# A two-layer gated mixer on one core: the first network, its norms and the attention products moved into the scan of the next batch, and the next mixer's preparation placed between the gate and the second network's down products

## What is computed

```python
# layer 0, mixer: a selective scan over 512 positions, 512 channels, 16 states
x  = silu(conv4(in_proj(ctx)))              # 512 channels x 512 positions
dt = softplus(dt_proj(x_proj(x)[:16]) + b)
state = state * exp(dt * A) + (dt * x) * B  # one sequential scan per channel and state
y  = sum_over_states(state * C) + D * x
x1 = x_in + tanh(g_x[0]) * y * silu(z)      # z is the layer norm of x_in
# layer 0, first network: 512 -> 2048 -> 512, weights of -1, 0, 1, inputs rounded to 8 bits
x2 = x1 + tanh(g_f[0]) * w2(round8(gelu(w1(round8(layernorm(x1))))))
# layer 1, attention over channels, its weights are made from ctx
x3 = x2 + tanh(g_x[1]) * layernorm(x2) @ attention.T
# layer 1, second network in fp32: 512 -> 2048 -> 512
out = x3 + tanh(g_f[1]) * (proj2(gelu(proj1(layernorm(x3)) + b1)) + b2)
```

## Time and profile before

| what | value |
|---|---|
| median of 3 runs | 1172.61 us (1170.66 to 1172.63) |
| the profiled execution | 1169.88 us, its span 1168.1 us |
| PE busy | 828.8 us (71%) |
| DVE busy | 904.9 us (77%) |
| ACT busy | 639.3 us (55%) |
| POOL busy | 563.9 us (48%) |
| mean granted TensorE clock | 0.844 of full speed |
| DMA | 130.07 MB, mean 111 GB/s |

### The profile page before, as it was taken

How to read it: one execution, slowest core, us unless ns; L and a number is a source line. 1 busy time by engine, 2 the same in 40 slices (tenths; PEclk the granted TensorE clock), 3 DMA queues, 4 the chain that set the end, 5 groups by cost and what they waited for, 6 DMA issues and landing times.

```text
span 1168.1 us, 10659 instructions
## 1 busy us (share of the span) xinstructions
PE 828.8 (71%) x2665; PEld 405.5 (35%) x2704; DVE 904.9 (77%) x1151; ACT 639.3 (55%) x889; POOL 563.9 (48%) x462
## 2 busy tenths in 40 slices
PE   5342311298598875899599877889498868887998
PEld 2010100143243332444234333344233323344886
DVE  3889988977888899687888899688878898565333
ACT  5556856467368843275488642365388641432442
POOL 0487568122777665123786674023877673123000
PEclk8565555599789997998799988998699988998999
DMA  7055995000168696220188786300287775200222
GB/s 249 0 106 110 218 260 100 16 1 1 43 139 176 147 228 152 94 86 36 29 173 177 159 199 162 128 0 36 45 179 162 164 185 146 90 1 1 91 91 72
DMA packets 51439, 130.07 MB, mean 111 GB/s; under 512 B 6304, under 2 KB 7456, under 8 KB 50864
## 3 DMA queue, kind: packets, MB, share of 16 engines
q0 software_dynamic: 17280, 62.92, 29.1%
q1 hardware_dynamic: 34096, 66.53, 16.9%
HBM read 62.33 MB, written 4.19 MB: 57 GB/s over the span
## 4 chain that ended last, share of the span: by engine, by line
PE 43%; DVE 22%; issue 12%; POOL 9%; DMA 7%; ACT 6%; POOLq 0%; DVEq 0%; ACTq 0%; SPq 0%; another core or an unknown queue 0%
PE bank L582 12%; DVE pair L1124 7%; PE bank L595 7%; DMA u<-work 6%; POOL work L1508 5%; PE bank L610 4%; PE pair L610 4%; PE pair L526 3%; PE pair L513 2%; PE bank L444 2%; DVE work L1128 2%; PE pair L571 1%; PE bank L452 1%; PE bank L469 1%; DVE u L1135 1%
## 5 line engine op out<-in xcount | busy, mean ns | idle before, releaser
L1124 DVE TENSOR_TENSOR_SCAN pair<-pair,work 128x512 f32<-128x512 f32 x256 | 313.0, 1223 | 49.1 <-ACT pair L797 42.7
L1508 POOL TENSOR_TENSOR work<-du,bcast 128x1024 f32<-128x1024 f32 x128 | 318.3, 2489 | 67.4 <-DMA u<-work 61.8
L797 ACT ACTIVATE pair<-dt,a_neg 128x512 f32<-128x512 f32 x256 | 168.1, 685 | 65.8 <-DVE work L1128 48.4
L582 PE MATMUL bank<-stage,ring 128*128 128x512 f32 x384 | 180.9, 615 | 22.2 <-ACT hx L979 8.0
L1128 DVE TENSOR_TENSOR work<-pair,ccast 128x512 f32<-128x512 f32 x256 | 177.0, 691 | 14.6 <-ACT bcast L782 1.4
L1519 POOL DMA_DIRECT2D u<-work x120 | 113.8, 950 | 81.2 <-DVE work L1128 74.6
L595 PE MATMUL bank<-ring,stage 128*128 128x512 f32 x192 | 94.5, 644 | 41.3 <-DVE stage L1365 39.9
L418 PE MATMUL bank<-xd,pick 128*128 128x512 bf16 x108 | 49.5, 458 | 96.8 <-ACT bcast L782 67.7
L582 PEld LDWEIGHTS bank<-stage,ring 128*128 128x128 f32 x384 | 74.3, 197 | 116.4 <-issue 89.8
L1554 POOL TENSOR_SCALAR stage<-stage,fst 128x2048 f32<-128x2048 f32 x16 | 33.1, 2067 | 119.8 <-DVE fst L1333 119.8
L782 ACT ACTIVATE bcast<-bank 128x512 f32<-128x512 f32 x64 | 38.0, 594 | 76.0 <-POOL work L1508 51.9
(11 more groups left out here) (158 smaller groups left out, 1578.6 us busy)
## 6 DMA issues: line engine op xcount, KB each, us to landing
u<-work POOLq DMA_DIRECT2D x120, 512.0 KB, 5.2
ring<-ffn_dram SPq DMA_DIRECT2D x144, 256.0 KB, 3.6
ring<-ffn_dram SPq DMA_DIRECT2D x16, 512.0 KB, 3.3
xres<-x_dram SPq DMA_DIRECT2D x4, 1024.0 KB, 5.4
stage<-w_dram SPq DMA_DIRECT2D x1, 4096.0 KB, 17.1
stage<-w_dram SPq DMA_DIRECT2D x4, 1024.0 KB, 8.4
out_dram<-stage SPq DMA_DIRECT2D x16, 256.0 KB, 2.8
ctxT<-ctxT_dram SPq DMA_DIRECT2D x4, 512.0 KB, 7.4
```

The costliest lines, as they stand in the source:

```text
L582: last = pe.matmul(banks[2 + f % 2][:], up_slot(f)[:, k * P:(k + 1) * P], xnT[:, k, :], start=k == 0, stop=k == J - 1)
L797: act.activation(pairs[s % DECAYBUFS][:, q, :], dt[:, p * HALF + q, :], ACT.Exp, scale=a_neg[:, p * HALF + q, n:n + 1]).then_inc(s_decay, 1)
L1124: dve.tensor_tensor_scan(state, state, row, 0.0, ALU.mult, ALU.add).then_inc(s_scan, 1)
L1508: pool.tensor_tensor(work[:, s % SCANBUFS, :, :], du[:, p * HALF:(p + 1) * HALF, :], bcast[:, n % 2, :].unsqueeze(1).broadcast_to([P, HALF ...
```

## The change

The tiles and the arithmetic stay; the order on each engine, and which PSUM banks are used, change. A pass is now `pass_(b, m, nxt)`. The part called `chain` (first network, norms and attention products of batch b) stands at places (5, 0) to (8, 0), one or two steps behind each half step of the scan of batch m. The 16 `f_up` move to places (8, 2) to (12, 1), and the 16 `f_down` units to (12, 2), (12, 3) and 14 places of a new part, `end(b, m, nxt)`. `end` holds the gate of batch m, these units, and the preparation of batch nxt with both halves of its state 0, then `up1` and `gelu1` of block 0. `up1` has two banks in turn where it had three, and shares them with `transpose_h`, `norm_transpose` and `attend`. The passes are now: preparation of batch 0; scan of batch 0, whose `end` prepares batch 1; a loop of two passes; a pass with b = 2 and m = 3, whose `end` prepares nothing; and the last with batch 3 alone. `quantise` writes its normalised rows into `xn` and no longer into `ccast`.

```diff
-SCAN_SLOTS = {4: (0, None), 5: (1, 2), 6: (3, 4), 7: (5, 6), 8: (7, 8), 9: (9, 10), 10: (11, 12), 11: (13, 14), 12: (15, None)}
-QK_SLOT = 5
-ATT_SLOTS = {6: 0, 7: 1, 8: 2, 9: 3}
-ATT_LAST_SLOT = 10
+SCAN_SLOTS = {5: (1, 2), 6: (3, 4), 7: (5, 6), 8: (7, 8), 9: (9, 10), 10: (11, 12), 11: (13, 14), 12: (15, None)}
+QK_SLOT = 7
+ATT_SLOTS = {8: 0, 9: 1, 10: 2, 11: 3}
+ATT_LAST_SLOT = 12
 ZSTAT_SLOT = 10
 ZS_SLOT = 12
-GATE_SLOT = 13
-QUANT_SLOT = 14
+END_SLOT = 13
...
-ATT_BANKS = (4, 6, 7, 6)
-MEAN_BANK = 1
-DT_BANKS = (0, 1, 5, 6)
-
-FFN_UP = {(5 + f // 4, f % 4): f for f in range(FT)}
-FFN_DOWN = {(9, 0): (0, 0), (9, 1): (0, 2), (9, 3): (0, 4),
-            (10, 0): (0, 6), (10, 1): (0, 8), (10, 3): (0, 10),
-            (11, 0): (0, 12), (11, 1): (0, 14),
-            (12, 0): (1, 0), (12, 1): (1, 2), (12, 3): (1, 4),
-            (13, 0): (1, 6), (13, 2): (1, 8), (13, 3): (1, 10),
-            (14, 0): (1, 12), (14, 3): (1, 14)}
-FOURTH_SLOTS = {(11, 1): 0, (14, 1): 1}
+MEAN_BANK = 2
+DT_BANKS = (5, 6, 7, 4)
+PROJ_BANKS = (6, 7)
+GATE_BANKS = (1, 0, 4, 5)
+NORM_ORDER = (0, 1, 4, 2, 5, 3, 6, 7)
+
+FFN_UP = {at: f for f, at in enumerate([(8, 2), (8, 3)] + [(slot, place) for slot in (9, 10, 11) for place in range(4)]
+                                       + [(12, 0), (12, 1)])}
+FFN_DOWN = {at: (i // 8, i % 8 * 2) for i, at in enumerate([(12, 2), (12, 3)] + [(END_SLOT, i) for i in range(14)])}
...
                 if j == 0:
                     pe.wait_ge(s_ctx, b * 16 + 16)
                     if prev is not None:
-                        pe.wait_ge(s_x1, prev * T + T)
-                elif j == 1 and prev is not None:
-                    pe.wait_ge(s_qT, prev * T + T)
+                        pe.wait_ge(s_hc, (prev + 1) * HN * HALF)
                 elif j >= 2:
                     pe.wait_ge(s_inprojc, b * J + j - 1)
                 for k in range(KC):
-                    last = pe.matmul(banks[j % 2][:], ipw[:, k, j * P:(j + 1) * P], ctxT[:, k, :],
+                    last = pe.matmul(banks[PROJ_BANKS[j % 2]][:], ipw[:, k, j * P:(j + 1) * P], ctxT[:, k, :],
                                      start=k == 0, stop=k == KC - 1)
...
+                    if c >= 2 or t == 1:
+                        pe.wait_ge(s_gelu, b * T * FC + g - 1)
+                    elif t >= 2:
+                        pe.wait_ge((s_ev0, s_ev1)[c], b * T + t - 1)
+                    elif c == 0:
                         pe.wait_ge(s_x4, b * T + 1)
                     for k in range(J):
-                        last = pe.matmul(banks[4 + g % 3][:], qT[:, k, t * P:(t + 1) * P],
...
-                    pe.wait_ge(s_x2, b * T + T)
-                if t == T - 1:
-                    pe.wait_ge(s_x3, b * T + 2)
+                elif t < T - 1:
+                    pe.wait_ge(s_ev0, b * T + t + 2)
+                else:
+                    pe.wait_ge(s_x3, b * T + t)
                 for k in range(J):
-                    last = pe.matmul(banks[ATT_BANKS[t]][:], xnT[:, k, t * P:(t + 1) * P], attT[:, k, :],
+                    last = pe.matmul(banks[2][:], xnT[:, k, t * P:(t + 1) * P], attT[:, k, :],
                                      start=k == 0, stop=k == J - 1)
                 last.then_inc(s_xm, 1)
...
+            def chain(b, slot, place):
+
+                if (slot, place) == (5, 0):
+                    up1(b, 1)
+                if (slot, place) == (5, 1):
+                    transpose_h(b, 0)
+                    down1(b, 0)
+                if (slot, place) == (5, 2):
+                    up1(b, 2)
...
+                if (slot, place) == (6, 0):
+                    up1(b, 3)
                     norm_transpose(b, 0)
+                    attend(b, 0)
+                if (slot, place) == (6, 1):
...
+                units(0)
+                if m is not None:
+                    gate_transposes(m, (0, 1))
+                units(1)
+                if m is not None:
+                    gate_transposes(m, (2, 3))
+                if nxt is not None:
+                    project(nxt, m, 0)
+                    project(nxt, m, 1)
...
+                units(5)
+                if nxt is not None:
+                    if m is None:
+                        pe.wait_ge(s_const, const_wait)
+                        pe.wait_ge(s_ones, 2)
+                    low_rank(nxt, m)
...
+                units(7)
+                if nxt is not None:
+                    scan_bcast(nxt, 0, 0)
+                    scan_bcast(nxt, 1, 0)
+                units(8)
+                if nxt is not None:
+                    scan_bcast(nxt, 0, 1)
+                units(9)
+                if nxt is not None:
+                    scan_bcast(nxt, 2, 0)
+                    scan_bcast(nxt, 1, 1)
+                units(10, 11, 12, 13)
...
+            end(None, None, 0)
+            pass_(None, 0, 1)
+            with pe.Fori(0, B - 2) as i:
+                pass_(i, i + 1, i + 2)
+            pass_(B - 2, B - 1, None)
+            pass_(B - 1, None, None)
...
+                    softplus(nxt, m)
+                    first_copy(nxt, m, 0, 0)
+                    first_copy(nxt, m, 1, 0)
+                if m is not None:
+                    q_copy(m, 3)
+                if nxt is not None:
+                    first_copy(nxt, m, 0, 1)
+                    decays(nxt, 0, 0)
+                    copy_bc(nxt, 2, 0)
+                    copy_bc(nxt, 1, 1)
+                    decays(nxt, 0, 1)
+                if m is None:
+                    weights(4)
+                if m is not None:
...
+            def chain(b, slot, place, last):
+
+                if (slot, place) == (5, 0):
                     dve_f.start()
-                if scans:
+                    h_scale(b, 0)
+                if (slot, place) == (5, 1):
+                    h_quant(b, 0)
+                    h_scale(b, 1)
+                if (slot, place) == (5, 2):
+                    h_quant(b, 1)
+                if (slot, place) == (5, 3):
+                    second(b, 0)
+                    h_scale(b, 2)
...
+            def end(b, m, nxt):
+
+                if m is not None:
+                    gate(m, 0)
+                    if b is None:
+                        weights(END_SLOT)
+                    gate(m, 1)
+                    for t in range(T):
+                        first_sum(m, t)
+                if nxt is not None:
+                    convolve(nxt, 0)
+                if m is not None:
+                    quantise(m, 0)
...
+                if b is not None:
+                    fourth(b, 0)
...
+                    softplus_max(nxt)
+                    softplus_tmp(nxt)
+                    softplus_sum(nxt, 0)
+                    softplus_sum(nxt, 1)
+                    half_step(nxt, 0, 0)
+                    half_step(nxt, 0, 1)
+                if b is not None:
+                    fourth(b, 1)
```

More of the change, by code:

```diff
@@ new lines, in chain @@
+                if (slot, place) == (6, 2):
+                    h_quant(b, 3)
+                    norm_apply(b, 4)
+                    second(b, 2)
+                if (slot, place) == (6, 3):
+                    third(b, 1)
+                    norm_apply(b, 2)
+                if (slot, place) == (7, 0):
+                    norm_apply(b, 5)
+                    second(b, 3)
+                if (slot, place) == (7, 1):
+                    third(b, 2)
+                    norm_apply(b, 3)
```

797 lines of the change are left out of this document (355 added, 442 removed).

## The result

| | before | after |
|---|---|---|
| median | 1172.62 us | 1287.28 us (1286.81 to 1290.51) |
| ratio | | 1.0988, 95% interval 1.0967 to 1.1009 |
| span of the profiled execution | 1168.1 us | 1285.0 us |
| mean granted TensorE clock | 0.844 | 0.836 |

The account below looks back on a forecast made before the run. No engine is full; the limit changes by stage. Stretch changes of -45.0, +94 in scans, -74, +37.0 and +4.5 put +16.4 on 1168.0 us, a 1184.4 span; with time around it and the median offset, 1189 us, range 1160 to 1220.

Parts of the forecast that it names:

- What bounds the kernel, and the cuts: Whole span: no engine full, limit changes by stage; cut at each scan's end and first half step of state 1.
- First end, last end, start and tail: Batch 1's preparation after a scan 71.6 us; batch 3's gate with units 69.5; opening 208.4; closing second network 94.4.
- DVE floor of S, 155 us: State 1 to scan's end, three times: DVE's 120.1 us scan plus 34.9 network work; with waits 169, ends 161 to 180.
- New waits inside the network are small when I follow block by block: Network inside the scan: only two new waits found, 0.7 us at first h_scale and 0.8 at last second.
- ScalarE pays 7.7 us beside DVE work, and I cost it at nothing: Each scan: six gelu1-related table loads of 1.28 us, hidden beside DVE work; 7.7 us if that cover is gone.
- 6 us for GpSimd: Each scan: norm_apply and h_quant slowed when meeting GpSimd in memory, 6 us taken from a possible 0 to 22.8.
- ScalarE holds the decays: In scans, ScalarE waits for TensorE before decays; six of twelve places cost 2.1 us, time 1227; chance 0.13.
- the floor: Rival: DVE never waits in a scan except three table waits, scan stretch 161 us, total 1165; chance 0.22.
- the case of no net effect: Whole kernel: gains of 119 us and losses of 136 cancel if a tenth of losses fails, 1172; chance 0.07.
- The signs named beforehand: Forecast wrong if scans stay under 163 us, or scan's end to next state 1 is far over 87.
- C, 82 us: Scan's end to next state 1, twice: TensorE bound, 74.8 us work plus waits of 4, 2 and 1.5; ends 76 to 87.
- Network alone, 69.5: Batch 3's network by itself: shared banks 2 and 3 make it 69.5 us in place of 65.0, ends 65 to 73.

Follow-up runs that it names:

- a1: Changed kernel with each spread of the next place issued on TensorE ahead of the part that waits for ScalarE: 1261.2 us, ratio 1.0781.
- a2: Changed kernel with eight extra thrown-away products on TensorE between transpose_h and down1: 1266.7 us, ratio 1.0839.
- a3: Changed kernel with gelu1 as a scaling without Gelu, so no table load for it; computation left out: 1258.2 us, ratio 1.0735.
- c1: a1 with each down1 moved one place later, behind the h_copy of its block: 1247.4 us, ratio 1.0692.
- c2: c1 with units 10 and 11 issued ahead of two spreads in the stretch from scan's end to next state 1: 1234.6 us, ratio 1.0588.
- b1: Changed kernel with the first part of the change undone, all of chain running before slot 5 of the scan: 1319.1 us, ratio 1.1323.
- i2: c2 with norm_apply as two operations of two tensors, all operands in SBUF: 1251.9 us, ratio 1.0700.

## Why the prediction was wrong, point by point

- **What bounds the kernel, and the cuts:** right. First end, last end, start and tail came out within 4.2 us each. The two ends were sums over one engine with waits found by name; start and tail were carried over from the trace before.
- **DVE floor of S, 155 us:** right; DVE was busy 156.6 to 163.4.
- **"New waits inside the network are small when I follow block by block":** this is the step that failed. I followed `down1` to `second` and `gelu1` to `h_scale`, each block's own data. I did not follow the scan's data through the same queues: the spread behind `down1` on TensorE, its copy ahead of the decays on ScalarE, `h_copy` behind them. I had 0.7 and 0.8 us of new waits and 8.2 of idle time in all; the trace has 33 us idle in the network part. The edits that attack it, a1, a2, a3 and c1 (which contains a1), took 14, 7, 12 and 14 us off the second S. All in all c2 takes 43 of the 85.5 us off the three S, and leaving out the table loads 11 more; the last 31, some 10 per S, no run took away.
- **"ScalarE pays 7.7 us beside DVE work, and I cost it at nothing":** wrong twice; there are seven loads, 9.0 us, and S was 10.0 shorter without them (a3). The price had been named for the case that the cover is gone, and in the relay it was.
- **TensorE's clock in S:** no term for it. `down1` took 5.3 to 6.6 us in the second S in place of 3.6. The fillers brought 8 us per S back.
- **6 us for GpSimd:** near enough as work: VectorE's busy time is 2 to 8 us over the floor in after, and in c2 `norm_apply` takes 12.4 instead of 4.4 us. How much of it is on the path in after no run shows. As a rival for the whole gap it falls by that busy time, and by c2, whose S is 18 us shorter with longer hold-ups.
- **Rival "ScalarE holds the decays":** the nearest in kind, since it let ScalarE wait for TensorE before the decays; I had given it 0.13. It was priced at 2.1 us for six of twelve places, a row in which ScalarE only loads a table. The waits of ScalarE here are 5.5 to 7.0 us, because they hold a whole `down1` or `attend`.
- **The other rivals and the signs:** the floor and the case of no net effect needed shorter scans than the forecast and fall with S of 194 to 200. The signs named beforehand, S under 163 or C far over 87, did not include the way it came: S over its upper end of 180 three times.
- **C, 82 us:** the mechanism was right, the term mis-sized. TensorE in the first C, around the two spreads:

```profile
529.14 0.39 PE L416 MATMUL bank<-xd,pick 128*128 128x512 bf16 x1 [3.87 <-ACT bcast L792]
529.37 5.29 PE L589 MATMUL bank<-ring,stage 128*128 128x512 f32 x8
...
542.34 0.39 PE L416 MATMUL bank<-xd,pick 128*128 128x512 bf16 x1 [3.82 <-ACT bcast L792]
542.57 8.73 PE L589 MATMUL bank<-ring,hT 128*128 128x512 f32 x16
```

  The first wait is the 4 predicted. The second is 3.8, not 2, and behind each the next units run at the lower clock, 1.6 and 1.7 us longer than the 3.65 and 7.03 that as many products take elsewhere in this C.
- **Network alone, 69.5:** 74.9, and 75.4 in b1. With two banks, `transpose_h`, `h_copy` (2.0 us) and `down1` stand in line. VectorE is as busy there as before, 41.5 us; its waits before `third` for the attention product grew from 4.4 to 12.1 us, and those before `h_scale` for `gelu1` from 4.5 to 9.1. No run tests which of the shared banks makes them.
- **Open too:** how much of the last 14 us of S in c2 (183 on average against 169) is GpSimd's hold-up. No run took it away; i2 only shows that adding to it costs. And `up1` with two PSUM banks instead of three: in the part with the network TensorE stood 12.1 us for `gelu1` before a chunk of `up1` in the second S of after, and no run gave the third bank back.

## What to carry to other kernels

When work is moved beside other work, walk the orders of two engines that feed each other, not one block's data: for each wait of engine A on B, ask what stands ahead of the awaited instruction in B's order, and what that in turn waits for. If the answer comes back to A, the two take turns, and busy shares of all engines stay low while the time grows. What helps is to issue the small thing that the other engine needs first (here one spread of 0.4 us) ahead of the large one; the price of a term such as a table load can be nothing under cover (the first S of c2) and full in a relay (10.0 us for seven loads of 1.28).

## What the runs showed of the hardware

- Eight more products before each `down1`, thrown away, shortened the kernel by 1.4% (1.0988 to 1.0839); `down1` went from 6.15 to 3.61 us at the place shown, and the second S from a granted clock of 0.86 to 0.90.
- A product of two tensors of 128x512 on VectorE took 0.69 us with an operand in PSUM, in each of the 60 in the second S of c2 (0.691 to 0.692), 14 of which lie wholly inside a GpSimd product. The same operation with all operands in SBUF took 0.69 as a rule and up to 3.4 us (i2). `norm_apply`, all in SBUF, was held up in each of the three forms tried.
- `h_scale`'s maximum reads 2048 columns from SBUF and writes one: its 16 records in c2 took 2.27 to 2.29 us, and so did the one at 577.39 us in after that overlaps a GpSimd product.
